# A second graph layer on one core: a seventh unit in seven products, and the small steps of its layer norm on GpSimd

## What is computed

```python
deg = sum(adj, axis=1) + 1e-5
h = (adj / deg) @ x @ Wn.T + bn + x @ Ws.T + bs
x = layernorm(x + relu(h))                      # first layer
d = where(rowsum > 0, rowsum ** -0.5, 0)
h = (d[:, None] * adj * d[None, :]) @ x @ W + b
out = layernorm(x + relu(h))                    # second layer; layernorm without weights, eps 1e-5
```

## Time and profile before

| | us |
|---|---|
| median of 3 runs | 777.92 (777.8 to 778.35) |
| the profiled execution | 778.69 |
| its span, first to last instruction | 777.0 |
| TensorE busy in it | 769.2 (99%) |
| VectorE busy | 692.2 (89%) |
| ScalarE busy | 425.1 (55%) |
| GpSimd busy | 2.5 |
| granted TensorE clock, mean | 0.999 of full |

### The profile page before, as it was taken

One profiled execution on the slowest core, in us unless ns is written; L12 is line 12 of the kernel. 1 busy time (PEld: TensorE's weight loads), 2 busy tenths in 40 slices (PEclk: granted clock), 3 DMA queues, 4 the chain that ended last, 5 costly groups with the idle time before them and its releaser, 6 DMA issues.

```text
span 777.0 us, 12364 instructions
## 1 busy us (share of the span) xinstructions
PE 769.2 (99%) x4052; PEld 659.7 (85%) x4052; DVE 692.2 (89%) x1157; ACT 425.1 (55%) x583; POOL 2.5 (0%) x14
## 2 busy tenths in 40 slices
PE   9999999999999999999999999999999999999996
PEld 5888888888888888888888889898988989888886
DVE  6999999999899899998979899897989889796654
ACT  5644645646445464454554667556575755656452
POOL 0000000000000000000000000000000000000000
PEclk9999999999999999999999999999999999999999
DMA  8975574755647557374574756657575655757541
GB/s 301 337 240 200 191 254 157 244 190 197 238 152 243 189 173 259 135 271 165 186 254 139 246 188 227 223 183 235 181 248 180 226 204 180 238 178 253 190 143 55
DMA packets 54205, 161.08 MB, mean 207 GB/s; under 512 B 5024, under 2 KB 18080, under 8 KB 54176
## 3 DMA queue, kind: packets, MB, share of 16 engines
q1 hardware_dynamic: 45680, 151.54, 57.2%
q10 hardware_dynamic: 8352, 9.05, 3.6%
q0 software_dynamic: 144, 0.13, 0.2%
HBM read 152.31 MB, written 8.39 MB: 207 GB/s over the span
## 4 chain that ended last, share of the span: by engine, by line
PE 99%; DVE 0%; ACT 0%; issue 0%
PE ps_main L1085 75%; PE ps_epi L964 7%; PE ps_epi L1032 5%; PE ps_main L1023 3%; PE ps_main L1032 2%; PE ps_epi L1023 2%; PE ps_main L1107 1%; PE ps_main L964 1%; PE ps_main L1060 1%; PE ps_main L1045 1%; PE ps_epi L1117 0%; DVE tt L625 0%; PE ps_epi L985 0%; DVE tt L641 0%; ACT ps_epi L513 0%; ACT tt L527 0%
## 5 line engine op out<-in xcount | busy, mean ns | idle before, releaser
L361 ACT ACTIVATE hi<-raw 128x1024 fp32r<-128x1024 f32 x254 | 260.6, 1028 | 215.0 <-PE ps_main L1085 150.3
L569 DVE TENSOR_TENSOR lo<-raw,hi 128x1024 fp32r<-128x1024 f32 x254 | 299.8, 1183 | 36.3 <-ACT hi L361 35.8
L1085 PE MATMUL ps_main<-hi,xs 128*128 128x512 f32 x1120 | 278.8, 391 | 0.0
L1085 PEld LDWEIGHTS ps_main<-hi,xs 128*128 128x128 f32 x1120 | 207.4, 188 | 41.7 <-issue 0.5
L1085 PE MATMUL ps_main<-lo,xs 128*128 128x512 f32 x560 | 149.7, 389 | 0.0
L1085 PE MATMUL ps_main<-hi,zs 128*128 128x512 f32 x592 | 147.4, 391 | 0.0
L854 DVE TENSOR_TENSOR acc<-acc,raw 128x1024 f32<-128x1024 f32 x112 | 136.5, 1219 | 0.0
L1085 PEld LDWEIGHTS ps_main<-hi,zs 128*128 128x128 f32 x592 | 108.5, 188 | 20.9
L1085 PEld LDWEIGHTS ps_main<-lo,xs 128*128 128x128 f32 x560 | 105.1, 188 | 21.9
L1085 PE MATMUL ps_main<-lo,zs 128*128 128x512 f32 x296 | 79.1, 389 | 0.0
L1085 PEld LDWEIGHTS ps_main<-lo,zs 128*128 128x128 f32 x296 | 55.6, 188 | 11.5
(11 more groups left out here) (157 smaller groups left out, 747.9 us busy)
## 6 DMA issues: line engine op xcount, KB each, us to landing
raw<-adj_t SPq DMA_DIRECT2D x256, 512.0 KB, 3.4
res<-x_nat SPq DMA_DIRECT2D x11, 512.0 KB, 5.9
xt_sb<-xt SPq DMA_DIRECT2D x8, 512.0 KB, 5.5
x_scratch<-tt ACTq DMA_DIRECT2D x8, 512.0 KB, 3.9
res<-x_scratch SPq DMA_DIRECT2D x8, 512.0 KB, 5.1
out<-tt ACTq DMA_DIRECT2D x7, 512.0 KB, 6.9
tt<-x_nat SPq DMA_DIRECT2D x3, 512.0 KB, 4.3
acc<-x_nat ACTq DMA_DIRECT2D x1, 512.0 KB, 5.1
```

The source lines that it names most:

```text
L361: return act.activation(dst, src, ACT.Copy)
L569: return dve.tensor_tensor(dst, src, hi_part.bitcast(f32), ALU.subtract)
L1085: last = pe.matmul(ps[:, f, :], stationary(layer, part, jt, f), mov[:, slot(u), cols], start=(jt == 0 and i == 0), stop=(jt == JT - 1 and ...
```

## The change

SU gets unit 12 as a seventh member. With that the ring of split sums `S` in `xs` has three places instead of two (SRING), the sums in `acc` still two, so that the sums of a unit wait until the low part of the unit two before it in SU is written (`sl_ready`); and T_UNITS gets a fourth group, at unit 14, which holds unit 13 alone (its `t_sums` are behind the lo of unit 13). GpSimd gets a loop over the seven epilogues that run inside blocks 1 to 7 of the second layer: the negated means, the root's argument, the refining of the reciprocal in four steps, and mean times reciprocal. The reciprocal itself stays on VectorE, at the same place. Three semaphores carry the hand-over (`added`, `root_inverted`, `pool_chain`). The first layer's epilogues and the one at the end keep their steps on VectorE.

```diff
-SU = (1, 5, 7, 9, 11, 13)
+SU = (1, 5, 7, 9, 11, 12, 13)
 NS = len(SU)
 SUMS_AT = tuple(max(u - 2, 0) for u in SU)
-SRING = 2
+SRING = 3
 T_AT = XC + FH
 T_UNITS = tuple(range(5, 5 + 3 * ((NS + 1) // 2), 3))
@@ gpsimd
+            def moments(e):
+
+                r, q, a = inv_root[:, 0:TB], newton[:, 0:TB], root_in[:, 0:TB]
+                for pair in range(2):
+                    at = slice(2 * pair, 2 * pair + 2)
+                    pool.wait_ge(added, e * TB + 2 * (pair + 1))
+                    pool.tensor_scalar(nmean[:, at], sums[:, at], -1.0 / F, None, ALU.mult).then_inc(mean_ready, 1)
+                pool.wait_ge(squares_ready, e * TB + (NB + 1) * TB)
+                pool.tensor_scalar(a, squares[:, :], 1.0 / F, EPS_NORM, ALU.mult, ALU.add).then_inc(root_ready, 1)
+                pool.wait_ge(root_inverted, e + 1)
+                pool.tensor_tensor(q, a, r, ALU.mult).then_inc(pool_chain, 1)
+                pool.wait_ge(pool_chain, e * 4 + 1)
+                pool.tensor_tensor(q, q, r, ALU.mult).then_inc(pool_chain, 1)
+                pool.wait_ge(pool_chain, e * 4 + 2)
+                pool.tensor_scalar(q, q, -0.5, 1.5, ALU.mult, ALU.add).then_inc(pool_chain, 1)
+                pool.wait_ge(pool_chain, e * 4 + 3)
+                pool.tensor_tensor(r, q, r, ALU.mult).then_inc(pool_chain, 1)
+                pool.wait_ge(pool_chain, e * 4 + 4)
+                pool.tensor_tensor(nmr[:, :], nmean[:, :], r, ALU.mult).then_inc(norm_ready, 1)
+
+            for e in range(NB - 1):
+                moments(e)
@@ vector, s_sums
+                if SU.index(u) >= 2:
+                    dve.wait_ge(sl_ready, g - 1)
@@ vector, epilogue
-                    if p == 2:
-                        add_residual(n, w - 5)
-                if w in (7, 9) and p == 1:
-                    negate_means((w - 7) // 2)
-                if (w, p) == (11, 0):
+                    if p == 2 and layer == 0:
+                        link(add_residual(n, w - 5))
+                    if p == 2 and layer == 1:
+                        add_residual(n, w - 5).then_inc(added, 1)
+                if (w, p) == (11, 2) and layer == 1:
+                    dve.wait_ge(root_taken, n + 1)
+                    dve.reciprocal(rstd, root[:, 0:TB]).then_inc(root_inverted, 1)
+                if layer == 1:
+                    return
+                if v in (7, 9) and p == 1:
+                    negate_means((v - 7) // 2)
+                if (v, p) == (11, 0):
```

More of the change, by code:

```diff
@@ L128, in build @@
         own_ready = sem("own_ready")
+        added, pool_chain, root_inverted = sem("added"), sem("pool_chain"), sem("root_inverted")
         own_zeroed, u_chain, c_ready = sem("own_zeroed"), sem("u_chain"), sem("c_ready")
@@ L207, in build, with s_index, s_sums_of, s_part @@
         own_sbuf = xt
-        def s_index(b, parity, u):
+        def s_index(b, u):
             return b * NS + (SU.index(u) - NS)
-        def s_slot(parity, u):
-            return ((0 if parity == 1 else NS) + SU.index(u)) % SRING
+        def s_sums_of(parity, u):
+            return acc[:, (SU.index(u) + 1 - parity) % 2, :]
         def s_sum(parity, u, i):
-            return acc[:, s_slot(parity, u), i * HB:(i + 1) * HB]
-        def s_part(part, parity, u):
-            at = S_AT + s_slot(parity, u) * 4 + part * 2
+            return s_sums_of(parity, u)[:, i * HB:(i + 1) * HB]
+        def s_part(part, u):
+            at = S_AT + SU.index(u) % SRING * 4 + part * 2
             return xs[:, at:at + 2].rearrange("p a c f -> p (a c f)")
@@ L393, in s_hi @@
             def s_hi(b, parity, u):
-                act.wait_ge(s_ready, s_index(b, parity, u) + 1)
-                split_hi(s_part(0, parity, u), acc[:, s_slot(parity, u), :]).then_inc(sh_ready, 1)
+                act.wait_ge(s_ready, s_index(b, u) + 1)
+                split_hi(s_part(0, u), s_sums_of(parity, u)).then_inc(sh_ready, 1)
             def square_tiles(layer, e, parity, pair):
@@ L549, in _ @@
             layers(act, one_block, last_epilogue)
-        LINKS = (5 + 2 + 2 * TB + 4, 1 + TB + 4)
+        LINKS = (5 + 2 + 2 * TB + 4, 1)
         @block.vector
@@ L640, in add_residual @@
                 dve.wait_ge(tile_read, n * TB + (t + 1))
-                link(dve.scalar_tensor_tensor(out=tt[:, t, :], in0=tt[:, t, :], scalar=0.0, in1=res[:, t, :],
-                                              op0=ALU.max, op1=ALU.add, accum_out=sums[:, t:t + 1]))
+                return dve.scalar_tensor_tensor(out=tt[:, t, :], in0=tt[:, t, :], scalar=0.0, in1=res[:, t, :],
+                                                op0=ALU.max, op1=ALU.add, accum_out=sums[:, t:t + 1])
             def negate_means(pair):
@@ L652, in root_argument, with newton_step @@
                    .then_inc(root_ready, 1)
-            def newton_step(layer, n, step):
-                m = 2 * TB if layer == 0 else TB
-                r, q, a = inv_root[:, 0:m], newton[:, 0:m], root_in[:, 0:m]
+            def newton_step(n, step):
+                r, q, a = inv_root[:, :], newton[:, :], root_in[:, :]
                 if step == 0:
                     dve.wait_ge(root_taken, n + 1)
-                    link(dve.reciprocal(r, root[:, 0:m]))
+                    link(dve.reciprocal(r, root[:, :]))
                 if step == 1:
@@ L669, in newton_step, with norm_scales @@
                     link(dve.scalar_tensor_tensor(out=r, in0=q, scalar=1.5, in1=r, op0=ALU.add, op1=ALU.mult))
-            def norm_scales(layer, e):
+            def norm_scales(e):
                 linked()
[L673 to L677, removed]
+                r_sum = inv_root[:, TB:2 * TB]
+                dve.tensor_tensor(d_cur[:, :], r_sum, pos[:, :], ALU.mult)
+                dve.tensor_tensor(d_all[:, bass.ds(e * TB, TB)], r_sum, pos[:, :], ALU.mult)
                 dve.tensor_tensor(nmr[:, :], nmean[:, :], rstd, ALU.mult).then_inc(norm_ready, 1)
@@ L739, in s_sums @@
                 k0 = b * (NU // RING) + NB * (NU // RING)
-                g = s_index(b, parity, u)
+                g = s_index(b, u)
                 _, a22, a11, a21 = [raw[:, slot(u), i * HB:(i + 1) * HB] for i in range(4)]
                 s1, s2, s3 = [s_sum(parity, u, i) for i in range(3)]
+                if SU.index(u) >= 2:
+                    dve.wait_ge(sl_ready, g - 1)
                 dve.wait_ge(raw_full[slot(u)], (k0 + (u // RING + 1)) * 16)
@@ L749, in s_last_sum @@
             def s_last_sum(b, parity, u):
-                dve.wait_ge(s_chain, s_index(b, parity, u) * 3 + 3)
+                dve.wait_ge(s_chain, s_index(b, u) * 3 + 3)
                 dve.tensor_tensor(s_sum(parity, u, 3), raw[:, slot(u), 0:HB], s_sum(parity, u, 1), ALU.subtract)\
@@ L754, in s_lo @@
             def s_lo(b, parity, u):
-                dve.wait_ge(sh_ready, s_index(b, parity, u) + 1)
-                split_lo(s_part(1, parity, u), acc[:, s_slot(parity, u), :], s_part(0, parity, u)).then_inc(sl_ready, 1)
+                dve.wait_ge(sh_ready, s_index(b, u) + 1)
+                split_lo(s_part(1, u), s_sums_of(parity, u), s_part(0, u)).then_inc(sl_ready, 1)
             def epilogue(layer, e, parity, v, p):
@@ L782, in epilogue @@
                         add_second(w - 5)
-                    if p == 2:
-                        add_residual(n, w - 5)
-                if w in (7, 9) and p == 1:
-                    negate_means((w - 7) // 2)
-                if (w, p) == (11, 0):
-                    root_argument(n)
[L789 to L794, removed]
+                    if p == 2 and layer == 0:
[10 more added lines that the diff above has]
+                if (v, p) == (11, 0):
+                    root_argument(n)
+                if (v, p) == (11, 2):
+                    newton_step(n, 0)
+                if v == 12:
+                    newton_step(n, p + 1)
+                if (v, p) == (13, 0):
+                    norm_scales(e)
                 if v == 15 and layer == 0:
@@ L883, in scaled_rows @@
                     scale_product(layer, n, t + 1, ps_epi[:, t + 1, :])
-                    add_residual(n, t)
-                    add_residual(n, t + 1)
+                    link(add_residual(n, t))
+                    link(add_residual(n, t + 1))
                 def spreads():
@@ L1000, in seven_products @@
             def seven_products(b, parity, u, g0):
-                g, s = SU.index(u), s_index(b, parity, u)
+                g, s = SU.index(u), s_index(b, u)
                 first, last_s = u == SU[0], u == SU[-1]
@@ L1029, in seven_products @@
                         pe.wait_ge(sl_ready, s + 1)
-                    mov = s_part((0, 0, 1)[i], parity, u)
+                    mov = s_part((0, 0, 1)[i], u)
                     for n, (ps, st, at) in enumerate(summed):
```

## The result

The changed kernel takes 782.07 us (median of 5 runs, 781.64 to 783.3) where the kernel before took 777.96 in the same session: a ratio of 1.0049, interval 1.0038 to 1.0061. It is slower by 4 us; forecast were 777.4, and 776.4 to 778.4.

A forecast was written before the change was run, and what follows sets the result against it. TensorE was taken to bound the kernel (99% of the last chain). Saving 1.32 us from unit 12 and adding a 0.80 us stall in block 0 gave -0.52 us: median 777.92 to 777.40, range 776.4 to 778.4.

The forecast's parts named there:

- the sign that it named itself: Prediction is wrong if TensorE shows idle time in blocks 1 to 6 of the second layer, or none in block 0.
- (a): Unit 12 of blocks 1 to 6 in seven products: TensorE saves 0.22 us a block, 1.32 us in all.
- (d): Fourth group of T sums in block 0: ScalarE's norm 0.98 us late, TensorE stalls 0.80 us ahead of unit 14.
- (b): VectorE's share of unit 12: net +1.7 us a block, covered by its 6 us lead over TensorE; no cost on the path.
- (c): Layer norm's small steps on GpSimd: 0.25 us each, 1.3 us for five behind the reciprocal; no cost on the path.
- The rival that I gave 0.07: GpSimd's chain in the second layer held up behind VectorE's long instructions: slower, 780.9 to 784.4 us; chance 0.07.
- The two rivals on the fast side: Block 0's stall doesn't come: 776.60 us, chance 0.15. Unit 12 isn't cheaper: 778.72 us, chance 0.06.

The follow-up runs named there:

- the late split: Changed kernel with block 0's fourth T group split later, behind unit 15's z tiles on ScalarE and z_lo on VectorE: 1.0042 to the kernel before, 782.27 us.
- unit 12 alone: Unit 12 in seven products as in the changed kernel, but all small norm steps on VectorE at their places of before: 0.9989 to the kernel before.
- GpSimd alone: Changed kernel without the seventh unit (six units, three T groups), small norm steps on GpSimd: 0.9997 to the kernel before, 778.44 us against 778.77.

## Why the prediction was wrong

By the sign that it named itself the prediction is wrong: TensorE waits in blocks 1 to 6. Two of its parts hold, (a) and (d), and two steps failed, in (b) and (c).

(a) *The saving of unit 12* was right: 45.12 us a block, three units of seven products in a row with starts 2.51 and 2.52 apart.

(d) *The fourth T group* was right in place, size and course. Changed kernel, block 0, timeline of ScalarE, VectorE and TensorE:

```profile
437.94 0.63 ACT L385 ACTIVATE xs<-acc 128x512 fp32r<-128x512 f32 x1 [0.34 <-DVE acc L750]
...
438.48 1.08 ACT L432 ACTIVATE tt<-tt,nmr,inv_root 128x256 f32<-128x256 f32 x2
...
442.08 0.48 DVE L705 SCALAR_TENSOR_TENSOR xs<-tt,d_cur,xs 128x256 fp32r<-128x256 f32 x1
442.61 1.69 PEld L1116 LDWEIGHTS ps_main<-hi,xs 128*128 128x128 f32 x8 [0.87 <-DVE xs L705]
442.61 2.12 PE L1116 MATMUL ps_main<-hi,xs 128*128 128x512 f32 x8 [0.44 <-DVE xs L705]
...
443.59 0.79 DVE L705 SCALAR_TENSOR_TENSOR xs<-tt,d_cur,xs 128x256 fp32r<-128x256 f32 x2
```

Unit 13 started at 439.29, unit 14 at 442.61, 0.60 late, and unit 15 at 445.49, 0.16 more: 0.76, against 0.80 forecast. The 0.16 is no second wait: z_lo of tiles 2 and 3 ended at 444.38, over 1 us ahead of unit 15. It comes from the first matmul of unit 14, which is drawn from the start of its weight load; that load stands 3.32 us behind unit 13's start (442.61 - 439.29), where it stood 2.50 behind it before (442.75 - 440.25), so 0.82 late. The term was right as a wait, and too dear in the sum: with a slower loop elsewhere about half of it cost nothing, as the late split showed.

(b) *"In units 10 to 13 it falls back by at most 2 us of its 6 ... and catches up there"* is a step that failed. The 6 us are a stock that must be refilled in every block. I compared busy time with the block (41.5 of 45.1, which is what it measured) and took the idle times ahead of units 14 and 15 for free time to catch up in. But VectorE can't work ahead there: it waits for ScalarE, and in the changed kernel 2.73 us ahead of unit 15 and 1.60 ahead of unit 0. The sum that was wanted is that of a turn: work 41.9 and waits 4.6, so 46.5 against 45.12. (In the kernel before VectorE's first turn took 44.45 us, from 479.52 to 523.98, and the next TensorE's 45.34.) In block 1 the reciprocal, in VectorE's list, already stood 33.6 us behind the start of TensorE's unit 0 where it had stood 31.1, so 2.5 later, and each turn added 1.4: after two more turns 5.3 of the 6 us were gone, and in block 3 TensorE began to wait.

(c) *"I take 0.25 us a step"* is the other. Two steps of the chain measured 0.20, three 0.82 to 1.06, and the chain 3.7 us instead of 1.3. The row nearest in kind (the select) had run at the start, with nothing beside it on VectorE. And the ceiling of "up to 1.5 us a step" asked only whether one block would reach TensorE. The rival that I gave 0.07 named the right mechanism, that steps are held up until VectorE's running instruction ends. A held step took no 0.25 us on top of that, but ended 0.04 to 0.06 behind the instruction. And the point that the rival had to pass, 7.4 us or 1.5 a step, was wrong: the chain was 2.4 us longer than forecast in every block, and that suffices where 7.4 in a single block would be needed. So "TensorE would still not wait" was wrong for the same reason. The turns add up now: with unit 12 alone 45.52; from the reciprocal's end to lo of unit 15 it is 579.05 - 574.37 = 4.68 us there and 580.92 - 575.08 = 5.84 in the changed kernel, 1.16 more; the steps ahead of the root, gone from VectorE, give back 0.2 (three of 0.07). 45.52 + 1.16 - 0.2 = 46.5, as measured. That the refining steps, moved too, gave nothing more back is read from this sum and not tested by a run of its own.

The two rivals on the fast side didn't come. Of the forecast, what holds is that part of the change that isn't GpSimd: unit 12 alone measured 0.9989 where the sum of (a), (b) and (d) gives 0.9993.

## What to carry to other kernels

An engine that runs ahead has a stock of time, not an allowance per block: add up one turn of the loop of engines (work, plus the waits each puts on the next) and compare it with the bound's turn. If it is longer, the bound engine pays as soon as the stock is spent, and the first blocks of the profile won't show it. Here 46.5 us against 45.12 was felt from the third block on, while 45.5 (unit 12 alone) lasted for all six. In a chain of tiny dependent steps given to GpSimd, each step that falls beside a busy VectorE can cost what is left of a VectorE instruction; steps for which nobody stands waiting cost nothing.

## What was not expected of the hardware

A GpSimd step on 4 columns takes 0.20 us beside an idle VectorE. Started during one of VectorE's instructions of 0.93 to 1.22 us, it ends 0.04 to 0.06 us behind it: 0.82 to 1.06 us in the changed kernel, up to 1.22 in the one with GpSimd alone (from 481.80). Started just ahead of VectorE's instruction it isn't held (GpSimd alone, block 3: 0.20 us from 569.29, VectorE's from 569.46). A write of a constant takes 0.10 us in either case. VectorE's instructions kept their 1.22 us. In TensorE's records the waiting was nearly invisible as idle time: blocks of 46.60 us, 1.48 too long, show 46.29 busy.
